# A fused decoder layer on one NeuronCore: four attention steps placed in the mixer's last part, and one causal mask made by GpSimd on the exponentials

## The chip, the core and the metric

The kernel runs on one NeuronCore of a Trainium2 chip. Five engines work side by side and meet at semaphores only: TensorE (PE, with its weight loads as PEld), VectorE (DVE), ScalarE (ACT), GpSimd (POOL) and SyncE (SP), which issues most of the DMAs. PE writes to PSUM; DVE and ACT read PSUM; POOL works on SBUF only. The metric is the device time of one execution in microseconds (us), and the number to predict is the median of the changed kernel.

## What is computed

One decoder layer for x of 8 x 256 tokens and 256 features, in float32:

```python
x = x + mixer(layernorm(x))                     # conv, gated recurrence, two gated linear maps
x = x + xattn(layernorm(x), ctx, ctx)           # 16 heads of 16
x = x + moe(layernorm(x))                       # 8 experts, top 2, capacity 641

# xattn, per batch element
scores = einsum('bhqd,bhkd->bhqk', q, k) * SCALE
scores = where(tril(ones(L, L)), scores, -inf)
probs  = softmax(scores)
out    = einsum('bhqk,bhkd->bhqd', probs, v) @ WO + bO
```

The mixer ends with `z = ssm * silu(ssm @ w2)` and `out = ssm + z @ w3`. The attention's queries come from the normalized x after the mixer, its keys and values from ctx.

## The kernel before

The program has two blocks. In each, every engine runs its own hand-written list, and a barrier of all engines stands between them.

**Block 1** (`mixer_and_projections`) takes the 2048 tokens in four blocks of 512 (`NBLK = 4`) in a loop over `i` in `range(NBLK + 2)`. Period `i` makes the recurrence, keys and values of token block `i`, the late mixer of block `i - 1` (`w2`, `gate_tanh`, `gate`, `w3`, `residual`, statistics, `normed`, `turn_q`), and the queries of block `i - 2`. The periods `i = 4` and `i = 5` have nothing new to start: they are the tail, in which only block 3's late mixer and the queries of blocks 2 and 3 are left. Matrices are split in a high and a low part, three matmuls each (`split_product`, L101). `q_high` and `biased_low` make the two parts of q, and SP stores q, k and v to DRAM (`store`, `store_v`).

**Attention** works on 16 groups g (a batch element and half its heads). `lay` loads a group's q and k from DRAM (four slots, `ITEMS`). A score unit `u = 3g + s` (48 in all) is `mask` (two matmuls, L246) and `scores` (L261) into `lead.sbanks[u % 2]`, then `maxima` on DVE (L275). After three units `turn_maxima` (L283 to L288) makes `mt`, SP stores it (`store_maxima`, L215), and `load_maxima` (L223) brings it back as two more rows of q. An attention step t then makes the scores again, turned, with the maxima taken off: `turned_mask` (L1589), `turned` (L1603) into `tbank`, `exps` on ACT (L1470) into `pr[t % 3]`, and one step later `weigh` (L1621) into `obank`. After three steps `invert` (L1839), `divide` (L1377) and `turn_back` follow, then `project` (L1641), the residual, the norm, the router and the scatter to the experts, each at a step that the tables in `attention_route_experts` name. Units run `LEAD = 6` ahead of steps: block 1's tail holds units 0 to 5, and block 2 runs `for t in range(END)` with step t and unit t + 6. Within a step the order on PE is

```python
turned_mask(t); mask(u); turned(t); scores(u); project; weigh(t - 1)
```

`turned_mask(t)` waits for `exps(t - 1)`, since there is one `tbank`. On SP, block 2 takes the groups in turn: `store_maxima(g)`, then `lay(g + 2)`, then the loads of weights and values. After the last step come the fetch of the scattered rows and the eight experts (PE nearly without a gap).

Of the kernel before, what the change touches and what calls it, by code (L numbers as in the profile page):

```python
# [14 lines left out]
P = 128  # L15
# [154 lines left out]
LEAD = 6  # L170
ITEMS = 4
# [4 lines left out]
class Lead:  # L176


    def __init__(self, nc, ctx):
# [5 lines left out]
        self.mt = [sb(f"mt{n}", [P, 32]) for n in range(2)]  # L185
        self.sbanks = [pb(f"scores{n}", [P, 8 * P]) for n in range(2)]
        piece = 4 * L
        self.q3 = [self.hi[:, n * piece:(n + 1) * piece].rearrange("p (h t) -> p h t", h=4) for n in range(ITEMS)]
        self.k3 = [self.lo[:, n * piece:(n + 1) * piece].rearrange("p (h t) -> p h t", h=4) for n in range(ITEMS)]
        self.v32 = [m[:, ITEMS * piece:(ITEMS + 1) * piece].rearrange("p (t v) -> p t v", t=2) for m in (self.hi, self.lo)]  # L190

# [46 lines left out]
def mask(pe, A, c, lead, u):  # L238

    ge(pe, A["nm"], u - 1)  # L240
    for e in range(2):
        bank = lead.sbanks[u % 2][:, e * 4 * P:(e + 1) * 4 * P]
        m = 4 if u % 3 == 0 else 2
        out = bank.rearrange("q (p k) -> q p k", p=m)
        out = out if u % 3 == 0 else out[:, :, P:2 * P]
        pe.matmul(out, c["identb"][:, :], c["mask"][:, :].unsqueeze(1).to_broadcast([P, m, P]),  # L246
                  start=True, stop=False, skip_group_check=True)


def scores(pe, A, lead, u):  # L250
# [6 lines left out]
    for p, e in todo:  # L257
# [3 lines left out]
        mm = pe.matmul(lead.sbanks[u % 2][:, at:at + keys], q[rows, p, tok], kx[rows, p, 0:keys], start=False,  # L261
# [4 lines left out]
def maxima(dve, A, lead, u):  # L266
# [3 lines left out]
    nm, sbank = lead.nm[g % 2], lead.sbanks[u % 2]  # L270
# [7 lines left out]
def turn_maxima(dve, A, own, lead, g):  # L278
# [9 lines left out]
    dve.transpose(lead.mt[g % 2][:, :], mx[:, :, :].rearrange("q n c -> q (n c)").bitcast(F32)).then_inc(A["mx"], 1)  # L288


def mixer_and_projections(nc, sems, c, lead, x_sb, bo, a, disp, qd, kd, vd, md):

    with ExitStack() as ctx:
# [16 lines left out]
        cv, th = sb("cv", [P, DC, BLK]), sb("th", [P, DC, BLK])  # L310
# [10 lines left out]
        vf = sb("vf", [P, TPB, HEADS * VP])  # L321
        banks = [m[:, n * BLK:(n + 1) * BLK] for m in lead.sbanks for n in range(2)] + [pb(f"bank{n}", [P, BLK]) for n in range(4, 8)]
# [33 lines left out]

        def pair(i, name, n):
            return banks[4 + 2 * ((len(PAIRS) * i + PAIRS.index(name)) % 2) + n]

# [9 lines left out]
        with nc.Block() as block:  # L369

            @block.sync
            def _(sp):
# [17 lines left out]
                def store(i, dst, sem, done):  # L390
                    sp.wait_ge(S[done], DC * (i + 1))
                    for e in range(2):
# [32 lines left out]
                for i in range(NBLK + 1):  # L425
# [6 lines left out]
                    if i < NBLK:  # L432
                        store(i, kd, "k_st", "kl")
                        store_v(i)
# [10 lines left out]
                lay(sp, A, S, lead, qd, kd, 1)  # L445
                load_values(sp, A, S, lead, vd, 0)
                lay(sp, A, S, lead, qd, kd, 2)
                lay(sp, A, S, lead, qd, kd, 3)
                load_values(sp, A, S, lead, vd, 1)
                store_maxima(sp, A, lead, md, 0)  # L450
                load_maxima(sp, A, lead, md, 0)
                sp.wait_ge(S["k_st"], 96 * NBLK)
# [4 lines left out]
            def _(pool):  # L457
# [37 lines left out]
                for i in range(NBLK + 2):  # L495
# [27 lines left out]
                    if i == 0:  # L523
                        other_constants(pool, S, c)

            @block.scalar
            def _(act):
# [71 lines left out]
                def ssm_high(i, m):  # L599
                    act.wait_ge(S["ssm"], DC * i + m + 1)  # L600
                    ge(act, S["q"], DC * i)
                    act.activation(xah[:, m, :], ssm[:, m, :], ACT.Copy).then_inc(S["ssmh"], 1)
# [33 lines left out]
                def q_high(i):  # L636
                    for m in range(DC):
# [22 lines left out]
                for i in range(NBLK + 2):  # L660
# [56 lines left out]
                    if last:  # L717
                        x2_high(i - 1)

            @block.tensor  # L720
            def _(pe):
# [60 lines left out]
                def w2(i):  # L782
# [5 lines left out]
                    ge(pe, S["ql"], DC * i)  # L788
                    for m in range(DC):
                        split_product(pe, pair(i + 1, "W2", m)[:, :], products("w2", m, (xah, xal))).then_inc(S["w2"], 1)  # L790

                def w3(i):
# [4 lines left out]
                    for n in range(2):  # L797
                        if i == NBLK - 1 and n == 1:
                            unit(2)
                        for j in range(2):  # L800
                            tok = slice((2 * n + j) * P, (2 * n + j + 1) * P)
                            out = pair(i + 1, "W3", n)[:, j * D:(j + 1) * D]
                            parts = []
                            for k in range(DC):
# [1292 lines left out]
```

## Time and profile before

| | us |
|---|---|
| median of 3 runs | 732.27 |
| lowest and highest | 730.75, 733.64 |
| the profiled execution | 739.06 |
| span of its instructions | 737.3 |
| PE / DVE / ACT / POOL busy | 626.5 / 501.1 / 350.2 / 333.7 |

Times in the rows below are us from the first instruction of the profiled execution, which was 6.8 us longer than the median of the runs. Block 1 without its tail ends at about 229, the tail at 269.2, the attention steps with PE's work at about 434, the last scatters at 457, and the experts fill the rest.

### The profile page before, as it was taken

How to read it: one execution, taken by the hardware profiler on the slowest of the kernel's cores; microseconds unless marked ns; L12 is line 12 of the kernel's file. 1: busy time of each engine (PE TensorE's matmuls, PEld its weight loads, DVE VectorE, ACT ScalarE, POOL GpSimd, SP SyncE). 2: the span in 40 equal slices, each digit the busy share in tenths (PEclk: the TensorE clock that was granted, in tenths of full speed). 3: DMA queues.
4: the chain of work that ended last, by engine and by line, in shares of the span. 5: the costliest groups of instructions: out<-in, count | busy, mean ns of one | idle time of the engine just before them, and what ended most of it. 6: DMA issues, size and time to landing. Idle time of an engine off the chain costs nothing.

```text
span 737.3 us, 11898 instructions
## 1 busy us (share of the span) xinstructions
PE 626.5 (85%) x4100; PEld 518.1 (70%) x4100; DVE 501.1 (68%) x1066; ACT 350.2 (48%) x683; POOL 333.7 (45%) x322
## 2 busy tenths in 40 slices
PE   3586998997987688889989851799999999999992
PEld 2465887876875554556555531799999999999992
DVE  5687688787696546666657262387888888788841
ACT  4565464662543024352343421356666666666551
POOL 1234424224240032112143367344868677686776
PEclk9798999999999669997788665699999999999997
DMA  9201403775317926556365410704263452521223
GB/s 295 83 3 43 128 29 89 274 203 139 90 44 198 211 64 164 133 141 163 83 162 142 160 38 17 254 22 152 25 170 68 127 153 43 168 31 17 28 29 44
DMA packets 63315, 81.64 MB, mean 111 GB/s; under 512 B 10295, under 2 KB 47938, under 8 KB 63256
## 3 DMA queue, kind: packets, MB, share of 16 engines
q1 hardware_dynamic: 53928, 72.85, 35.2%
q0 software_dynamic: 9216, 7.81, 7.4%
q8 instruction: 33, 0.54, 0.3%
q10 hardware_dynamic: 112, 0.23, 0.1%
q14 instruction: 26, 0.21, 0.1%
HBM read 48.27 MB, written 34.36 MB: 112 GB/s over the span
## 4 chain that ended last, share of the span: by engine, by line
PE 39%; issue 6%; DVE 5%; POOL 5%; DMA 4%; SPq 4%; ACT 1%; POOLq 0%; DVEq 0%; ACTq 0%
PE l_scores L101 13%; PE w_bank L1765 13%; DMA l_lo<-kd 3%; POOL out L1418 2%; PE a_out L1621 2%; SPq L208 2%; PE a_shared L1641 2%; POOL disp L1387 2%; PE l_scores L1699 2%; PE a_turned L1603 1%; PE l_scores L1722 1%; PE a_turned L1589 1%; PE l_scores L261 1%; DVE w_yt L1966 1%; DVE l_nm L275 1%
## 5 line engine op out<-in xcount | busy, mean ns | idle before, releaser
L1954 DVE SCALAR_TENSOR_TENSOR w_v<-w_th,l_scores 128x324 f32<-128x324 f32 x128 | 62.1, 490 | 55.1 <-ACT w_th L1509 53.8
L1509 ACT ACTIVATE w_th<-l_scores 128x324 f32<-128x324 f32 x128 | 56.4, 441 | 84.7 <-PE l_scores L101 83.8
L1405 POOL TENSOR_TENSOR l_lo<-w_v,l_hi 128x324 fp32r<-128x324 f32 x64 | 59.0, 922 | 75.0 <-ACT l_hi L1515 74.8
L1470 ACT ACTIVATE a_pr<-a_turned 128x1024 f32<-128x1024 f32 x48 | 49.1, 1023 | 89.1 <-PE a_turned L1603 87.2
L101 PE MATMUL l_scores<-l_hi,w_w1h 128*128 128x324 f32 x256 | 81.1, 317 | 2.3 <-DVE l_lo L1946 1.2
L1418 POOL DMA_INDIRECT out<-w_y,w_to x48 | 76.3, 1591 | 12.1 <-issue 9.7
L101 PE MATMUL l_scores<-l_lo,w_w1h 128*128 128x324 f32 x256 | 80.6, 315 | 0.0
L101 PE MATMUL l_scores<-l_hi,w_w1l 128*128 128x324 f32 x256 | 80.5, 314 | 0.0
L275 DVE TENSOR_REDUCE l_nm<-l_scores 128x4 f32<-128x1024 f32 (+1 forms) x48 | 58.3, 1215 | 31.7 <-PE l_scores L261 30.9
L1765 PE MATMUL w_bank<-l_hi,w_w2h 128*128 128x324 f32 x256 | 64.5, 323 | 2.2 <-DVE w_yt L1966 1.2
L1515 ACT ACTIVATE l_hi<-w_v 128x324 fp32r<-128x324 f32 x128 | 59.9, 472 | 12.4 <-DVE w_v L1954 11.7
L1928 DVE TENSOR_TENSOR w_w2l<-w_s,w_w2h 128x256 fp32r<-128x256 f32 x56 | 60.9, 1087 | 1.9
L1765 PE MATMUL w_bank<-l_hi,w_w2l 128*128 128x324 f32 x256 | 61.5, 311 | 0.0
L1765 PE MATMUL w_bank<-l_lo,w_w2h 128*128 128x324 f32 x256 | 61.5, 311 | 0.0
L1394 POOL TENSOR_TENSOR w_w1l<-w_s,w_w1h 128x256 fp32r<-128x256 f32 x64 | 55.1, 862 | 1.7 <-ACT w_w1h L1494 0.2
L1377 POOL TENSOR_TENSOR a_on<-a_po,a_rc 128x256 f32<-128x256 f32 x16 | 9.9, 620 | 98.0 <-DVE a_rc L1841 98.0
L101 PEld LDWEIGHTS l_scores<-l_hi,w_w1h 128*128 128x128 f32 x256 | 49.2, 192 | 2.9 <-ACT l_hi L1504 2.9
L101 PEld LDWEIGHTS l_scores<-l_hi,w_w1l 128*128 128x128 f32 x256 | 49.2, 192 | 0.0
L101 PEld LDWEIGHTS l_scores<-l_lo,w_w1h 128*128 128x128 f32 x256 | 49.1, 192 | 0.0
L101 PE MATMUL l_scores<-m_sh,l_hi 128*128 128x512 f32 x96 | 40.0, 416 | 10.3 <-ACT m_sh L565 6.9
L1765 PEld LDWEIGHTS w_bank<-l_hi,w_w2h 128*128 128x128 f32 x256 | 42.6, 189 | 4.1 <-issue 4.1
L1765 PEld LDWEIGHTS w_bank<-l_hi,w_w2l 128*128 128x128 f32 x256 | 43.7, 188 | 0.0
(253 smaller groups left out, 1587.0 us busy)
## 6 DMA issues: line engine op xcount, KB each, us to landing
w_s<-in_L_ffn_w SPq DMA_DIRECT2D x14, 1024.0 KB, 7.4
l_lo<-kd SPq DMA_DIRECT2D x32, 200.0 KB
l_hi<-qd SPq DMA_DIRECT2D x32, 192.0 KB
disp<-c_blank SPq DMA_DIRECT2D x8, 658.1 KB
w_rows<-disp SPq DMA_DIRECT2D x7, 658.1 KB
kd<-l_qkh SPq DMA_DIRECT2D x16, 256.0 KB, 4.7
vd<-m_vf SPq DMA_DIRECT2D x4, 1024.0 KB, 6.8
qd<-l_qkh SPq DMA_DIRECT2D x16, 256.0 KB, 3.9
```

The costliest lines, as they stand in the source:

```text
L101: mm = pe.matmul(out, a, b, start=first and n == 0, stop=last and n == 3 * len(parts) - 1)
L208: sp.dma_start(m[64 * e:64 * e + c, :, :].bitcast(F32), rows[k, e][:, :, b * L:(b + 1) * L])\
L275: dve.tensor_reduce(dst, src, AX.X, ALU.max).then_inc(A["nm"], 1)
L1394: pool.tensor_tensor(w1_piece(w1l, f), w1_piece(s1[e % 2], f), w1_piece(w1h, f).bitcast(F32), ALU.subtract)\
L1405: pool.tensor_tensor(hl[:, g % 3, half(1)], v[:, n % 4, :], hh[:, g % 3, half(1)].bitcast(F32), ALU.subtract)\
L1418: pool.indirect_dma_start(out=out, out_offset=bass.IndirectOffsetOnAxis(ap=to[:, e % 3, t:t + 1], axis=0), in_=y[e % 2][:, t, :], in_offse ...
L1470: act.activation(pr[n % 3][:, :], tbank[:, :], ACT.Exp, scale=SCALE).then_inc(A["exp"], 1)
L1509: act.activation(th[:, n % 2, :], hb[n % 2][:, 0:HALF], ACT.Tanh, scale=0.5).then_inc(F["th"], 1)
L1515: act.activation(hh[:, g % 3, half(u)], v[:, n % 4, :], ACT.Copy).then_inc(F["hh"], 1)
L1765: mm = pe.matmul(eb[2 * k + u][:, 0:HALF], w2_piece(w, f)[:, k * P:(k + 1) * P], a[:, g % 3, half(q)], start=f == 0 and n == 0, stop=f == ...
L1928: dve.tensor_tensor(w2_piece(w2l, f), w2_piece(s2[e % 2], f), w2_piece(w2h, f).bitcast(F32), ALU.subtract)\
L1954: dve.scalar_tensor_tensor(v[:, n % 4, :], th[:, n % 2, :], 1.0, hb[n % 2][:, 0:HALF], ALU.add, ALU.mult).then_inc(F["v"], 1)
```

## The change

- Four steps (`START = 4`) move into block 1's tail, and with them score units 6 to 9. Block 2 begins with step 4 and unit 10. `LEAD` stays 6.
- `turned_mask` is gone. Instead POOL zeroes what lies over the diagonal in the exponentials with an affine select (`cut`): 4 x 128 elements of each partition, and all 1024 in every third step. `weigh(n)` waits for `cut(n)` where it waited for the exponentials.
- The tail is written out by hand, in another order. Block 3's `w2` reads its input from `sh, sl`, which are free by then (before, from `xah, xal`, in which the queries of block 2 had to be done first), and the PSUM banks of the tail are dealt anew. Units 1, 3 and 5 use `tbank`, units 6 to 10 all use `sbanks[0]`.
- `pr`, `th`, `vf` and later `y` share one piece of SBUF (`area`), so that `exps(1)` waits for the store of the last values.
- SP lays groups 1 and 4 earlier, in block 1, and stores the q of block 2 in two halves around `load_maxima(0)`. The q of block 3 is stored in groups 4 and 5 of block 2, where it was the first thing of block 2.
- POOL's `with_bias` (four instructions of 128 x 1024 at the start of block 2) becomes 16 of 128 x 256, one to a step, and `base` is cut up in the same way. `cut(t)` stands first in POOL's list of step t.

```diff
+def turned(pe, A, lead, n):
+    ge(pe, A["exp"], n)
+    if n == 0:
+        pe.wait_ge(A["nm"], LEAD)
...
+def cut(pool, A, lead, n):
+    pool.wait_ge(A["exp"], n + 1)
+    own = lead.pr[n % 3][:, :].rearrange("k (m q) -> k m q", m=8 if n % 3 == 2 else 4)[:, :, 0:P]
+    pool.affine_select(out=own, in_=own, compare_op=ALU.is_ge, fill=0.0, base=0,
+                       pattern=[[0, own.shape[1]], [1, P]], channel_multiplier=-1).then_inc(A["cut"], 1)
...
 def weigh(pe, A, lead, n):
-                    pe.wait_ge(A["exp"], n + 1)
+    pe.wait_ge(A["cut"], n + 1)
...
-                for i in range(NBLK + 2):
+                for i in range(NBLK):
...
-                    if t < NS:
-                        turned_mask(t)
                     if u < NS:
                         mask(pe, A, c, lead, u)
                     if t < NS:
-                        turned(t)
+                        turned(pe, A, lead, t)
```

**PE in the tail.** In these rows `m_xah`, `m_xal` with `m_wh`, `m_wl` into two banks are a projection, L808 (L921 in the change) is `w3`, L727 (L838) is `turn_q`, and L246/L261 (L262/L277) are a score unit. Before, from the queries of block 2 to the barrier:

```order
L101 MATMUL m_bank<-m_xah,m_wh 128x512 [waits m_hs,m_xl2,m_xh2]
...
L246 MATMUL l_scores<-c_mask,c_identb 128x512 [waits m_ring]
...
L101 MATMUL m_bank<-m_xah,m_wh 128x512 [waits m_dx,m_ql,m_ssml,m_ssmh]
...
L808 MATMUL m_bank<-m_wh,m_zh 128x256 [waits m_zl,m_zh]
...
L246 MATMUL l_scores<-c_mask,c_identb 128x2x128 [waits a_nm]
...
L727 MATMUL m_bank<-c_ident,m_xn 128x128 [waits m_xn2,m_vf]
...
L101 MATMUL m_bank<-m_xah,m_wh 128x512 [waits m_hs,m_xl2,m_xh2]
...
L1577 UNCONDITIONAL_BRANCH [waits barrier_Pool_Activation_PE_DVE_SP_release]
```

The change, from `w2` of block 3 on:

```order
L101 MATMUL l_out<-m_sh,m_wh 128x512 [waits m_dx,m_vf,m_ssml,m_ssmh]
...
L921 MATMUL l_scores<-m_wh,m_zh 128x256 [waits m_ql,m_zl,m_zh]
...
L327 MATMUL l_turned<-l_hi,l_lo 128x256 [waits a_m_in0,a_nm]
L327 MATMUL l_turned<-l_hi,l_lo 128x256 x3
L838 MATMUL l_scores<-c_ident,m_xn 128x128 [waits m_xn2,m_vf]
...
L277 MATMUL l_scores<-l_lo,l_hi 128x128 [waits a_laid2]
...
L347 MATMUL l_out<-l_area,l_hi 32x256 [waits a_v_in0,a_cut]
L347 MATMUL l_out<-l_area,l_hi 32x256 x3
L101 MATMUL l_scores<-m_xah,m_wh 128x512 [waits m_xl2,m_xh2]
...
L347 MATMUL l_out<-l_area,l_hi 32x128 [waits a_cut]
```

`w2` no longer waits for the low part of block 2's queries (`m_ql`), and step 0 stands ahead of `turn_q`.

**PE in one attention step.** Before (names: `a_turned` is `tbank`, `a_out` is `obank`):

```order
L1589 MATMUL a_turned<-c_identb,c_mask 128x512 [waits a_exp]
L1589 MATMUL a_turned<-c_identb,c_mask 128x512
L246 MATMUL l_scores<-c_mask,c_identb 128x2x128 [waits a_nm]
L246 MATMUL l_scores<-c_mask,c_identb 128x2x128
L1603 MATMUL a_turned<-l_hi,l_lo 128x128 x8
L261 MATMUL l_scores<-l_lo,l_hi 128x256 x4
L1621 MATMUL a_out<-a_pr,l_hi 32x256 [waits a_exp]
```

The same step in the change:

```order
L262 MATMUL l_scores<-c_mask,c_identb 128x2x128 [waits a_nm]
L262 MATMUL l_scores<-c_mask,c_identb 128x2x128
L327 MATMUL l_turned<-l_hi,l_lo 128x128 [waits a_exp]
L327 MATMUL l_turned<-l_hi,l_lo 128x128 x7
L277 MATMUL l_scores<-l_lo,l_hi 128x256 x4
L347 MATMUL l_out<-l_area,l_hi 32x256 [waits a_cut]
```

The wait for the exponentials has moved behind `mask(u)`, and `weigh` waits for POOL.

**POOL in the steps of the change**, from the start of block 2:

```order
L1517 TENSOR_TENSOR a_on<-a_po,a_rc 128x2x8x16 [waits a_po]
L357 AFFINE_SELECT l_area<-l_area 128x4x128 [waits a_exp]
L1503 TENSOR_TENSOR g_x<-g_x,g_bo 128x256
L357 AFFINE_SELECT l_area<-l_area 128x1024 [waits a_exp]
L1503 TENSOR_TENSOR g_x<-g_x,g_bo 128x256
L357 AFFINE_SELECT l_area<-l_area 128x4x128 [waits a_exp]
L1503 TENSOR_TENSOR g_x<-g_x,g_bo 128x256
L1517 TENSOR_TENSOR a_on<-a_po,a_rc 128x2x8x16 [waits a_o,a_po]
```

Before, four additions of the bias stood here and no select.

## Rows read from the trace of the kernel before

**Rows 1.** Busy us (count) of PE, PEld, DVE, ACT, POOL by stage; clock, DMA share, GB/s.
```profile
229.10:269.20 40.10, 28.51 (x128) 21.48 (x129) 22.89 (x44) 8.70 (x13) 1.01 (x2) 0.74 0.62 154
269.20:434.50 165.30, 148.62 (x1330) 89.76 (x1330) 100.84 (x269) 64.77 (x87) 51.95 (x56) 0.82 0.53 136
434.50:463.10 28.60, 5.39 (x23) 4.17 (x23) 8.85 (x57) 2.40 (x6) 23.11 (x23) 0.53 0.15 44
```

**Rows 2.** PE in order of time: start us, us, what [idle before <-releaser].
```profile
234.91 0.47 PE L101 MATMUL m_bank<-m_xah,m_wh 128*128 128x512 f32 x1 [1.01 <-DVE m_xal L944]
...
242.15 0.55 PE L808 MATMUL m_bank<-m_wh,m_zh 128*128 128x256 f32 x1 [4.22 <-DVE m_zl L944]
...
257.09 2.21 PE L727 MATMUL m_bank<-c_ident,m_xn 128*128 128x128 f32 x8 [3.70 <-DVE m_xn L1020]
...
260.75 0.77 PE L101 MATMUL m_bank<-m_xah,m_wh 128*128 128x512 f32 x1 [0.31 <-issue]
...
269.22 0.58 PE L1589 MATMUL a_turned<-c_identb,c_mask 128*128 128x256 bf16 x2 [2.37 <-PEq L369]
...
280.67 0.39 PE L1589 MATMUL a_turned<-c_identb,c_mask 128*128 128x256 bf16 x2
```

**Rows 3.** DVE in order of time, in the tail.
```profile
228.96 0.69 DVE L914 TENSOR_TENSOR m_ssm<-m_ssm,m_dx 128x512 f32<-128x512 f32 x1
...
252.38 0.69 DVE L1013 TENSOR_TENSOR g_x<-m_bank,g_x 128x512 f32<-128x512 f32 x1 [3.18 <-PE m_bank L813]
```

**Rows 4.** Windows, columns as in group 1.
```profile
237.00:241.00 4.00, 0.93 (x5) 0.42 (x3) 2.97 (x5) 1.74 (x4) 0.00 (x0) 1.00 0.96 226
241.00:245.00 4.00, 2.85 (x13) 2.88 (x14) 2.13 (x3) 0.28 (x1) 0.00 (x0) 0.60 0.90 206
...
257.00:265.00 8.00, 7.61 (x27) 5.03 (x28) 5.14 (x8) 1.88 (x3) 0.00 (x0) 0.50 0.15 50
341.00:357.00 16.00, 16.00 (x107) 9.10 (x100) 9.28 (x32) 4.80 (x7) 1.31 (x2) 0.50 0.44 110
```

**Rows 5.** SP's queue in order of time, at the start of block 2.
```profile
283.81 3.72 SPq L1340 DMA_DIRECT2D w_wo<-in_L_xattn_WO  x8
```

**Rows 6.** The chain that ended last, in order of time, between two waits for keys.
```profile
317.31 0.73 DVE a_po L1839
...
323.69 0.56 SPq L215
...
326.47 5.15 DMA l_lo<-kd
```

**Rows 7.** PE in order of time: two waits for laid keys.
```profile
295.46 0.67 PE L261 MATMUL l_scores<-l_lo,l_hi 48*128 48x128 f32 x8 [1.00 <-DMA l_lo<-kd]
...
314.08 0.66 PE L261 MATMUL l_scores<-l_lo,l_hi 48*128 48x128 f32 x8 [0.86 <-DMA l_lo<-kd]
```

**Rows 8.** PE in order of time: one step at the full clock, one mask at half.
```profile
304.89 0.39 PE L1589 MATMUL a_turned<-c_identb,c_mask 128*128 128x256 bf16 x2 [0.26 <-ACT a_pr L1470]
305.12 0.59 PE L246 MATMUL l_scores<-c_mask,c_identb 128*128 128x512 bf16 x2
...
306.47 0.64 PE L1621 MATMUL a_out<-a_pr,l_lo 128*32 128x128 f32 x16
...
348.43 1.03 PE L1589 MATMUL a_turned<-c_identb,c_mask 128*128 128x512 bf16 x2
```

**Rows 9.** POOL's groups of lines: busy us, mean ns of one.
```profile
L1362 POOL TENSOR_TENSOR g_x<-g_x,g_bo 128x1024 f32<-128x1024 f32 x4 | 9.3, 2363 | 0.0
...
L142 POOL MEMSET c_blank<- 108x1560 f32 x1 | 1.4, 1412 | 0.0
...
L136 POOL TENSOR_SCALAR_AFFINE_SELECT c_ident<-c_ident 128x128 f32<-128x128 f32 x1 | 0.3, 288 | 0.2 <-POOL c_ident L134 0.2
```

**Rows 10.** POOL in order of time, the same subtraction twice.
```profile
208.15 1.67 POOL L476 TENSOR_TENSOR m_gl<-m_acc,m_gh 128x512 fp32r<-128x512 f32 x1
...
216.63 1.28 POOL L476 TENSOR_TENSOR m_gl<-m_acc,m_gh 128x512 fp32r<-128x512 f32 x1 [0.52 <-ACT m_gh L591]
```

More of the change, by code:

```diff
@@ L170 @@
 LEAD = 6
+START = 4
 ITEMS = 4
@@ L185, in __init__ @@
         self.mt = [sb(f"mt{n}", [P, 32]) for n in range(2)]
+        self.area = sb("area", [P, 3 * 8 * P])
+        self.pr = [self.area[:, n * 8 * P:(n + 1) * 8 * P] for n in range(3)]
         self.sbanks = [pb(f"scores{n}", [P, 8 * P]) for n in range(2)]
+        self.tbank, self.obank, self.shared = pb("turned", [P, 8 * P]), pb("out", [P, 4 * P]), pb("shared", [P, 4 * P])
         piece = 4 * L
@@ L524, in _ @@
                         other_constants(pool, S, c)
+                for t in range(START):
+                    cut(pool, A, lead, t)
             @block.scalar
@@ L891, in _ @@
                         turn_q(i - 1)
-                    if i == NBLK:
-                        unit(4)
                     if now:
                         mixed(i, 1)
+                unit(0)
+                unit(1)
+                queries(NBLK - 2, (0,))
+                w2(NBLK - 1)
+                queries(NBLK - 2, (1,))
+                unit(2)
+                unit(3)
+                w3(NBLK - 1, 0)
+                unit(4)
+                w3(NBLK - 1, 1)
+                unit(5)
+                step(0)
+                turn_q(NBLK - 1)
+                unit(6)
+                step(1)
+                weigh(pe, A, lead, 0)
+                queries(NBLK - 1)
+                step(2)
+                unit(7)
+                weigh(pe, A, lead, 1)
+                step(3)
+                unit(8)
+                weigh(pe, A, lead, 2)
+                unit(9)
             @block.vector
@@ L1091, in _ @@
                         delta(i, 2)
-                    if last and not now:
-                        for m in range(DC):
-                            last_low("ssml", xal, ssm, xah, "ssmh", i - 1, m)
-                    if i == NBLK:
-                        maxima(dve, A, lead, 0)
                     if i + 1 < NBLK:
@@ L1109, in _ @@
                         dmin(i, 3)
-                    if last and not now:
-                        for m in range(DC):
-                            last_low("zl", zl, z, zh, "zh", i - 1, m)
-                    if i == NBLK:
-                        maxima(dve, A, lead, 1)
                     if now:
@@ L1443, in _ @@
                 low_w1(0, FC - 1)
-                base(NBLK - 2)
-                base(NBLK - 1)
+                for t in range(TPB * (NBLK - 2), NT):
+                    base(t)
                 low(0)
@@ L1973, in result @@
                         .then_inc(F["y_dve"], 1)
-                for t in range(END):
+                invert(0)
+                for t in range(START, END):
                     u = t + LEAD
```

333 lines of the change are left out of this document (189 added, 144 removed).

## The prediction

> **What bounds the kernel now.** I read the windows by stage first, then PE in order of time through the tail, then the chain that ended last through the attention steps, then POOL's groups. The windows [rows 1] show three stages that the change can touch. In the tail PE is busy 28.5 of 40.1 us at a mean clock of 0.74. In the attention steps it is busy 148.6 of 165.3 us at 0.82. In the routing's end, 28.6 us, POOL is busy 23.1 and PE 5.4. The experts behind that get the same work in the same order; I leave them as they are.
>
> PE in the tail [rows 2] is bound by a chain through all engines: `w2` waits for the low part of ssm (starts at 234.91), `w3` for the low part of z (242.15, after 4.22 us idle), `turn_q` for the normalized x (257.09, after 3.70), the last queries start at 260.75, and block 2 starts at 269.22. Step 4 starts at 280.67. So the first four steps stand on this path with 280.67 - 269.22 = 11.45 us, while the tail has holes of about that size.
>
> The clock matters there. PE was nearly idle from 237 to 241, the clock went from 1.00 to a mean of 0.60 in the next four us, and at 0.50, which is 1.2 GHz, eight us of nearly full PE work still ran from 257 to 265 [rows 4]. `w3` and its residual took 242.15 to 253.07, or 10.9 us [rows 2, 3].
>
> In the attention steps the chain that ended last does not run through PE alone. It passes DVE (the turn of `obank`, x, statistics, two maxima) from 317.31, SP's store of the maxima at 323.69 and then four lay DMAs whose last takes 5.15 us, to 331.6 [rows 6]. PE waits for such keys until 295.46 and until 314.08, 1.00 and 0.86 us [rows 7]. Other cycles are bound by PE itself: from 341 to 357 it is busy 16.00 of 16.00 us at half clock [rows 4].
>
> **The change, part by part.**
>
> *The tail's front.* The last sum of ssm ends at 228.96 + 0.69 = 229.65 [rows 3]. Its high part on ACT and its low part on DVE are instructions of about 0.65 us each (128 x 512, as the 0.69 of that row), so both are there at about 231.1. `w2` in the change waits for these and no longer for block 2's queries, of which half (six matmuls) stand ahead of it on PE; I start it at 231.3, which is 234.91 - 231.3 = 3.6 us earlier. From `w2` to `w3` it took 242.15 - 234.91 = 7.2 us; the same steps follow each other, so `w3` starts at 238.6.
>
> *`w3` at the full clock.* PE's hole before `w3` is now filled by half the queries and units 2 and 3, with 1 to 1.5 us idle left. The clock had held through 241 with four us of near-idleness, so I take `w3` and units 4 and 5 at 2.4 GHz. The 10.9 us go to about 6.4 (40 matmuls and a unit at half their time, and 0.69 of residual): x is done at 245.0, 8.1 us earlier.
>
> *Norm and turn.* From x to `turn_q` it took 257.09 - 253.07 = 4.0 us. In the change one `maxima` and `turn_maxima` stand on DVE ahead of the normalization, of which some 0.6 us is not covered by POOL's power: 249.7. Step 0 needs the same maxima and fits in this hole.
>
> *The work put in.* `turn_q` and half a us of copies take 2.2 at half clock (PE has been idle from 244.8 to 248.5). Then unit 6, step 1 and `weigh(0)` stand ahead of the last queries: about 1.8 + 0.8 + 1.1. They start at 255.5 where they started at 260.75: 5.2 of the 8.1 us are left. The queries are 12 matmuls, 2.8 us at 2.4 GHz and 5.1 at 1.2. Behind them q's two parts (0.7 each), and a strict alternation of PE and DVE, because units 7, 8 and 9 share one bank: `maxima(7)`, unit 8, `maxima(8)`, unit 9, `maxima(9)`, which is 3 x 1.2 + 2 x 1.1 with the gaps. The sum is 255.5 + 4.0 + 1.4 + 5.8 = 266.7. All at the full clock it would be 265.7, all at half 270.3. Step 4 starts at 266.8 where it started at 280.67: **13.9 us**, with ends at 10.4 and 15.
>
> SP must follow. In block 2 it issues the first weights, the maxima of group 2, the 3.72 us of WO [rows 5], and only then lays group 5: 266.7 + 1.1 + 0.6 + 4.2 + 0.6 + 2.9 + 5.1 = 281.2 for the scores of unit 15. (1.1 and 0.6, 0.5 and 0.6 are its short issues, 2.9 and 5.1 the lay.) In the trace this was at 295.46, after 1.00 us of waiting [rows 7], so the 14 us stand. PE waits here some 3 us now.
>
> *The masks of turned scores.* At the full clock the next instruction starts 305.12 - 304.89 = 0.23 us after one of 2 x 256 columns [rows 8], twice that for 2 x 512; at half clock twice as much again (the 1.03 us row). All 44 left in block 2 give 44 / 3 x 0.9 = 13 us at the full clock. But only cycles bound by PE can pay. Between two waits for keys of odd groups the path goes DVE, SP, DMA [rows 6], in which no mask stands: zero. I count the masks of twelve steps at half clock in two PE-bound cycles, 2 x 2.5, and 3 for the nine last steps, most of them held by other engines; less 2 us because the wait before unit 15 leaves the clock low. **6 us**, ends 0 and 10.
>
> *The select on POOL.* The trace has a select of 128 elements only: 0.288 us. A memset runs at 1.412 / 1560 = 0.9 ns an element, an addition of two inputs at 2.363 / 1024 = 2.3 [rows 9]. That puts 512 elements at 0.63 to 1.2 us, and 1024 at 1.1 to 2.4. I take 0.8 and 1.5, near the select's own row. The exponential's end to `weigh` on PE is 306.47 - 304.89 + 0.26 = 1.8 us before, of which the two masks leave (about 0.75): 1.1 in the change. The short select is done in time, the long one costs 0.5 us of PE's wait in every third step. It is partly covered, since `turned(t + 1)` waits for the exponential of step t anyway. I take zero beyond what the range holds. The Trainium skill, "GPSIMD Engine Reference", section "Performance versus the Vector engine", gives about 1.8 cycles an element as the best case of a loop with one input, 0.77 us for 512; as an estimate that would be 1.5 us for 1024, and the sum by it is the same. No row here has that size.
>
> *`with_bias` and `base` in pieces, q stored later, keys 1 and 4 earlier.* POOL is busy 52 of 165 us in the steps [rows 1]; 44 selects add about 45, with room. The additions of bias go from 9.3 us in one piece to 16 pieces, of which one stands between two selects. SP's stores of q moved behind two lays: nobody waits until group 12. Zero each; uncovered, a late select would cost PE its length.
>
> *Sum.* 739.06 - 13.9 - 6 = 719.2 for a profiled execution. This one was 6.8 us over the median, and rows do not tell where. If the median run has no half clock in `w3`, 4.5 us of my gain are not there; I take half of that back: 732.27 - 19.9 + 2.2 = **714.5 us**.
>
> **Rivals.** *The lay chain takes the masks' gain.* PE gets faster and waits as much longer for keys. For it: the waits [rows 7], and the 8 us from `turn_maxima` to the scores hold no PE work [rows 6]. Against: the sixteen us of saturated PE [rows 4]. 714.5 + 5 = 719.5.
>
> *The tail is longer.* The clock falls in the hole before step 0 and stays at half through units 6 to 9: block 2 starts at 270.3, 3.5 us later, and step 0 waits for the round trip of the maxima, about 2 more: 720.
>
> *The port.* The same subtraction on POOL took 1.67 us beside a DVE scan and 1.28 without [rows 10]. A select that is stretched by 0.4 us in each group's long step costs 16 x 0.3 = 5 us: 719. The Trainium skill, "SBUF — State Buffer", section "Who interferes with whom", says that a DVE instruction with two SBUF inputs and a GpSimd one shut each other out for their whole length. The trace agrees in size, but in the steps DVE reads mostly PSUM.
>
> *Slower: the select holds PE and takes its clock.* If 1024 elements cost 2.4 us, `weigh` waits 1.4 us in every third step, PE loses the density that keeps 2.4 GHz, and the groups that now run at full clock (about eight, 7.1 us each) run like those at half (11 less the masks' 1.7, so 9.4): +18 us; projections and the rest of these steps +5. Less the 14 us of the tail and without the masks' 6: 732.3 - 13.9 + 23 = 741. It decides from about 2 us for the long select. Against it: the 0.288 us row.
>
> *The change does not do it* (steps 0 to 3 wait in the tail for their maxima and push it back by as much): 11.45 us return, only some masks stay: 728.
>
> **How the numbers follow.** Forecast 0.55, lay chain 0.14, long tail 0.13, port 0.06, no effect of the tail 0.06, slower 0.06. The forecast's own ends: 732.27 - 15 - 10 = 707 and 732.27 - 10.4 - 2 + 4.5 = 724. The rivals to 720 lie inside; I go to 705 and 727. Half a per cent, 3.7 us, is about what a measurement can tell from no change: 728.6 is the bound. Faster 0.91, same 0.03, slower 0.06.
>
> **What would show it.** Right: `w2` at 231 to 232; `w3` at 238 to 240 at a clock of 1.00 with x done by 246; block 2's first PE work at 266 to 270 with step 4; long selects of 1.2 to 1.8 us; PE's waits for `kd` longer than before; the experts' length unchanged. Wrong: a PE wait on POOL as a leading row of the waits; block 2 starting after 272; a granted clock in the steps well below 0.82.

## The result, and the profile after

The changed kernel takes **747.4 us** (median of 4 runs, 744.0 to 749.6) where the kernel before takes 732.5 in the runs beside it: the ratio is 1.020, with a 95% interval of 1.016 to 1.025. I had forecast 714.5, between 705 and 727. It is slower, and lies outside the range. The profiled execution took 749.57 us, its span is 747.8. Runs that were clearly longer than the others of their kernel, at a lower granted clock, are left out of the ratios; the profiled run of the kernel before (739.1) is one of them, so its rows are set below beside those of k7, the same kernel with one store moved, profiled at 730.1.

The windows by stage, columns as in [rows 1]:

```profile
229.10:268.30 39.20, 31.07 (x209) 21.62 (x206) 28.71 (x53) 13.48 (x17) 4.15 (x6) 0.87 0.65 163
268.30:443.50 175.20, 142.54 (x1142) 86.08 (x1142) 103.68 (x254) 60.72 (x83) 89.28 (x117) 0.66 0.47 124
443.50:472.00 28.50, 6.81 (x34) 5.41 (x30) 10.40 (x65) 2.40 (x6) 21.32 (x24) 0.56 0.09 24
```

The tail holds four steps more in 39.2 us, at a clock of 0.87 where it was 0.74. The attention steps, four fewer of them, take 175.2 us instead of 165.3, and the clock in them is 0.66 instead of 0.82. (From 268 to 343 and from 343 to 408 us it is 0.67 and 0.66; k7 has 0.89 and 0.87 there.) The routing's end is as long as before, and the experts behind it take 275.8 us instead of 274.2. Nearly the whole loss is in the steps.

PE through the tail, in order of time, as [rows 2]:

```profile
231.93 0.39 PE L101 MATMUL l_out<-m_sh,m_wh 128*128 128x512 f32 x1
...
239.07 0.36 PE L921 MATMUL l_scores<-m_wh,m_zh 128*128 128x256 f32 x1 [0.98 <-ACT m_zh L708]
...
249.07 0.50 PE L327 MATMUL l_turned<-l_hi,l_lo 50*128 50x256 f32 x4 [3.59 <-DVE l_nm L291]
250.12 2.21 PE L838 MATMUL l_scores<-c_ident,m_xn 128*128 128x128 f32 x8 [0.55 <-DVE m_xn L1155]
```

`w2`, `w3` and `turn_q` start within 0.7 us of the forecast (231.3, 238.6, 249.7), and in the windows from 237 to 249 the clock is 1.00. Block 2's first PE work, the mask of unit 10, stands at 268.27. The tail did what it was meant to.

The exponential of one step is a milestone that both kernels have. Steps 4, 24, 26, 37, 40 and 47, first in the kernel before, then in the changed one (ACT in order of time):

```profile
281.76 1.02 ACT L1470 ACTIVATE a_pr<-a_turned 128x1024 f32<-128x1024 f32 x1 [1.14 <-PE a_turned L1603]
343.66 1.02 ACT L1470 ACTIVATE a_pr<-a_turned 128x1024 f32<-128x1024 f32 x1 [4.12 <-PE a_turned L1603]
350.98 1.02 ACT L1470 ACTIVATE a_pr<-a_turned 128x1024 f32<-128x1024 f32 x1 [2.76 <-PE a_turned L1603]
392.56 1.02 ACT L1470 ACTIVATE a_pr<-a_turned 128x1024 f32<-128x1024 f32 x1 [2.13 <-PE a_turned L1603]
402.31 1.02 ACT L1470 ACTIVATE a_pr<-a_turned 128x1024 f32<-128x1024 f32 x1 [2.55 <-PE a_turned L1603]
429.07 1.00 ACT L1470 ACTIVATE a_pr<-a_turned 128x1024 f32<-128x1024 f32 x1
```

```profile
269.12 1.02 ACT L365 ACTIVATE l_area<-l_turned 128x1024 f32<-128x1024 f32 x1 [5.06 <-PE l_turned L327]
339.09 1.02 ACT L365 ACTIVATE l_area<-l_turned 128x1024 f32<-128x1024 f32 x1 [2.94 <-PE l_turned L327]
349.61 1.01 ACT L365 ACTIVATE l_area<-l_turned 128x1024 f32<-128x1024 f32 x1
390.06 1.03 ACT L365 ACTIVATE l_area<-l_turned 128x1024 f32<-128x1024 f32 x1 [1.69 <-PE l_turned L327]
410.81 1.02 ACT L365 ACTIVATE l_area<-l_turned 128x1024 f32<-128x1024 f32 x1 [6.07 <-PE l_turned L327]
437.77 1.00 ACT L365 ACTIVATE l_area<-l_turned 128x1024 f32<-128x1024 f32 x1
```

The lead is 12.6 us at step 4, 4.6 at step 24, 1.4 at step 26, 2.5 at step 37, and a lag of 8.5 at step 40 and 8.7 at step 47. Against k7, whose profiled run is at its median, the leads are 15.2 and 3.1 at steps 4 and 24, and the lags 2.7, 5.8, 16.7 and 16.9 at the other four: 32 us lost between step 4 and step 47, of which 12 by step 24. So there are two losses of different kinds: a slow one over the first twenty steps, and sharp ones near steps 26 and 39.

The sharp ones are read from PE's waits and from SP's queue. PE first, from 268 to 443 us (what waited <- what it waited for: us in total, times, longest):

```profile
PE l_turned L327 <- DMA l_hi<-md: 14.7, 5, 6.6
```

```profile
353.04 0.80 PE L327 MATMUL l_turned<-l_hi,l_lo 50*128 50x256 f32 x4 [5.03 <-DMA l_hi<-md]
...
402.58 0.80 PE L327 MATMUL l_turned<-l_hi,l_lo 50*128 50x256 f32 x4 [6.60 <-DMA l_hi<-md]
```

Step 27 waits 5.03 us for the maxima of group 9, step 39 later 6.6 for those of group 13. Now DVE (where those maxima are made), SP and POOL around it, in order of time:

```profile
338.08 0.21 DVE L304 STREAM_TRANSPOSE l_mt<-l_mx 128x32 f32<-128x32 f32 x1
```

```profile
345.38 0.39 SPq L1465 DMA_DIRECT2D out<-g_x  x1
345.81 0.57 SPq L231 DMA_DIRECT2D md<-l_mt  x1
```

```profile
334.91 0.73 POOL L1512 TENSOR_TENSOR g_x<-g_x,w_x 128x256 f32<-128x256 f32 x1
...
344.62 0.74 POOL L1512 TENSOR_TENSOR g_x<-g_x,w_x 128x256 f32<-128x256 f32 x1
```

The maxima are ready at 338.3 (338.08 and 0.21). SP stores them at 345.81, since `store_base(0)` stands ahead in its queue and waits for four pieces of `base`. The change dealt these pieces out to steps 22 to 25, one each (the first and the last stand above), and the last ends at 345.36. SP's wait for POOL there lasts 16.3 us, and the next such store is late too, at 394.53: the maxima of group 13, ready at 385.4, follow it at 394.97. In the kernel before, with `base` in one piece, SP issued that store at 339.64 and the maxima at 340.71.

The slow loss goes with the clock. Windows right behind the start of block 2, columns as in [rows 1]:

```profile
265.00:269.00 4.00, 1.93 (x18) 1.18 (x20) 2.93 (x6) 0.00 (x0) 0.19 (x1) 1.00 0.34 84
269.00:273.00 4.00, 4.00 (x37) 2.07 (x34) 2.94 (x4) 1.02 (x1) 1.95 (x3) 0.64 0.40 100
...
277.00:281.00 4.00, 4.00 (x32) 2.14 (x28) 2.74 (x5) 1.02 (x1) 2.69 (x5) 0.50 0.86 188
281.00:285.00 4.00, 4.00 (x30) 2.13 (x28) 2.52 (x4) 1.73 (x3) 2.46 (x3) 0.50 0.17 45
285.00:289.00 4.00, 4.00 (x16) 2.69 (x18) 1.23 (x1) 0.93 (x2) 1.32 (x2) 0.50 0.52 124
```

PE idled half of the four us up to 269; its clock fell to 1.2 GHz and stayed there from 273 to 289, although PE is busy nearly all of that time. A stretch like this is no proof by itself: k7, with its masks on PE, was granted 0.50 from 273 to 281 and 0.51 from 281 to 285 with PE busy 4.00 us in each window of four. The difference is in how often it happens, which the means over the steps show. The select itself is cheap (POOL's groups, busy us and mean ns):

```profile
L357 POOL TENSOR_SCALAR_AFFINE_SELECT l_area<-l_area 128x512 f32<-128x512 f32 x32 | 20.5, 642 | 28.0 <-ACT l_area L365 27.8
L357 POOL TENSOR_SCALAR_AFFINE_SELECT l_area<-l_area 128x1024 f32<-128x1024 f32 x16 | 17.5, 1093 | 25.4 <-ACT l_area L365 25.3
```

So two theories stood: **A**, SP's queue (the sharp losses), and **B**, the clock without the masks on PE (the slow loss). Within B it was open whether the added PE work counts or the new wait of `weigh` for POOL.

### The profile page after: what moved, and what is told of

Same layout as the page of the kernel before. It is cut to its first block, busy times and chain, and to the rows that moved or that the text cites. A ratio compares the mean times of both kernels' runs of the same rounds, so it can differ in the third digit from the quotient of the medians.

```text
span 747.8 us, 11802 instructions
## 1 busy us (share of the span) xinstructions
PE 626.7 (84%) x4004; PEld 517.2 (69%) x4004; DVE 511.0 (68%) x1066; ACT 353.1 (47%) x685; POOL 375.0 (50%) x394
## 4 chain that ended last, share of the span: by engine, by line
PE 39%; POOL 7%; DVE 6%; issue 6%; DMA 3%; ACT 1%; SPq 1%; POOLq 0%; ACTq 0%; DVEq 0%
PE l_scores L101 13%; PE l_turned L1857 6%; PE l_out L1857 3%; PE l_shared L1857 3%; PE l_shared L1733 2%; PE l_out L347 2%; POOL disp L1527 2%; POOL out L1558 2%; PE l_scores L1791 2%; DMA l_lo<-kd 2%; PE l_turned L327 2%; PE l_scores L277 1%; PE l_scores L1814 1%; POOL l_area L357 1%; PE l_scores L262 1%
## 5 line engine op out<-in xcount | busy, mean ns | idle before, releaser
L365 ACT ACTIVATE l_area<-l_turned 128x1024 f32<-128x1024 f32 x48 | 49.1, 1023 | 98.9 <-PE l_turned L327 95.8
L1558 POOL DMA_INDIRECT out<-l_area,w_to x48 | 76.2, 1588 | 12.1 <-issue 9.7
L291 DVE TENSOR_REDUCE l_nm<-l_scores 128x4 f32<-128x1024 f32 (+1 forms) x45 | 54.8, 1217 | 37.1 <-PE l_scores L277 37.0
L1654 ACT ACTIVATE l_hi<-w_v 128x324 fp32r<-128x324 f32 x128 | 59.9, 472 | 12.4 <-DVE w_v L2044 11.8
L357 POOL TENSOR_SCALAR_AFFINE_SELECT l_area<-l_area 128x512 f32<-128x512 f32 (+1 forms) x48 | 38.0, 792 | 53.4 <-ACT l_area L365 53.2
L327 PEld LDWEIGHTS l_turned<-l_hi,l_lo 50*128 50x128 f32 x256 | 24.5, 250 | 38.0 <-issue 29.1
L327 PE MATMUL l_turned<-l_hi,l_lo 50*128 50x256 f32 (+1 forms) x256 | 34.8, 382 | 18.3 <-DMA l_hi<-md 14.7
L101 PE MATMUL l_scores<-m_sh,l_hi 128*128 128x512 f32 x96 | 40.0, 417 | 10.3 <-ACT m_sh L657 6.9
L566 POOL TENSOR_TENSOR m_gl<-m_acc,m_gh 128x512 fp32r<-128x512 f32 x16 | 24.5, 1533 | 37.4 <-ACT m_gh L683 37.4
L557 POOL TENSOR_TENSOR m_rstd<-m_ve,c_mhalf 128x4 f32<-128x4 f32 (+1 forms) x7 | 8.3, 1189 | 62.7 <-DVE m_ve L118 62.7
L101 PE MATMUL l_scores<-m_sl,l_hi 128*128 128x512 f32 x96 | 39.2, 408 | 0.0
```

What stands on the lines that cost most here:

```text
L101: mm = pe.matmul(out, a, b, start=first and n == 0, stop=last and n == 3 * len(parts) - 1)
L291: dve.tensor_reduce(dst, src, AX.X, ALU.max).then_inc(A["nm"], 1)
L327: mm = pe.matmul(lead.tbank[:, at:at + w], kx[rows, p, key], q[rows, p, tok], start=True, stop=True, skip_group_check=True)
L365: act.activation(lead.pr[n % 3][:, :], lead.tbank[:, :], ACT.Exp, scale=SCALE).then_inc(A["exp"], 1)
L1558: pool.indirect_dma_start(out=out, out_offset=bass.IndirectOffsetOnAxis(ap=to[:, e % 3, t:t + 1], axis=0), in_=y[e % 2][:, t, :], in_offse ...
L1654: act.activation(hh[:, g % 3, half(u)], v[:, n % 4, :], ACT.Copy).then_inc(F["hh"], 1)
```

## The experiments

### First four: each suspect alone, and both

**k1_store_later**: the changed kernel, with the store one group later.

```
-                    if g % 4 == 0 and g >= 8:
+                    if g % 4 == 1 and g >= 9:
                         store_base(g // 4 - 2)
```

> The changed kernel with one thing moved: SP issues the two stores of the first 1024 output rows (store_base(0), store_base(1)) one group later (groups 9 and 13, behind that group's store of the maxima). Theory A, SP's queue: in the changed kernel store_base(0) waits until 345.38 for the fourth piece of base on POOL (16.3 us at the longest), and the store of the maxima of group 9, ready since 338.3, is issued at 345.81; the same at 394.97. Then the waits of PE for md of 5.03 and 6.60 us go, and the time falls from 747.4 by 10 to 13 us to 734-737. Theory B, the clock: PE at a mean clock of 0.66 is the bound through the steps and the waits for md only take the place of slower PE work; then 743-747.

Measured: **731.5** (10 runs, 726.4 to 736.1), ratio to before 1.000 (0.997 to 1.004). 15.8 us less than the changed kernel. SP, in order of time:

```profile
336.50 0.57 SPq L231 DMA_DIRECT2D md<-l_mt  x1
...
343.44 0.38 SPq L1465 DMA_DIRECT2D out<-g_x  x1
```

The maxima leave first, and PE's waits for `md` shrink (again from 268 to 443 us):

```profile
PE l_turned L327 <- DMA l_hi<-md: 3.5, 5, 1.2
```

Theory A holds, and is worth more than I expected (734 to 737). The waits for `md` are 11.2 us shorter; where the rest of the 15.8 comes from is not shown.

**k2_pe_masks**: the changed kernel, its masks of turned scores again on PE, no select.

```
-    pe.wait_ge(A["cut"], n + 1)
+    pe.wait_ge(A["exp"], n + 1)
...
-                    if t < NS:
-                        cut(pool, A, lead, t)
...
+                    if t < NS:
+                        turned_mask(pe, A, c, lead, t)
```

The same is done in the tail's four steps.

> The changed kernel with the causal mask of the turned scores back on PE (two bf16 matmuls a step, the turned scores accumulate onto them) and no select on POOL; weigh waits for the exponential. The tail with four steps stays, SP's order stays. Theory B, the clock: the dense bf16 columns give back the granted clock, the mean in the steps rises from 0.66 to 0.8 and the 8 us lost between step 4 and step 24 come back: about 739. Theory A, SP's queue: base is still in pieces that end at step 25, so the two long waits for md stay; PE has 48 x 0.3 to 0.8 us more work: 745-752.

Measured: **737.8** (8 runs, 734.4 to 739.2), 9.6 us less than the changed kernel, and the clock in the two windows is 0.89 and 0.72 where that kernel has 0.67 and 0.66. Theory B holds beside A, with its two halves (the work on PE, the wait for the select) still together.

**k3_both**: both edits.

> Both edits: SP's store of the base one group later, and the masks of the turned scores back on PE. If A and B both hold, the 12.4 us that the tail gained are all kept: 732.5 - 12 = 720 (718-724). If only A holds: 736-740, no better than the store alone. If only B holds: 739 as with the masks alone.

Measured: **719.8** (4 runs, 718.3 to 725.3), ratio 0.986 (0.981 to 0.992). Step 4's exponential is at 266.70 and the last at 408.63. It beats both kernels, and the two causes about add up: 15.8 and 9.6 one by one, 27.6 together.

**k4_cut_alone**: the kernel before with the select (and pieces, and the later store), its tail as it was.

```
+                    if t < NS:
+                        cut(t)
...
-                    if t < NS:
-                        turned_mask(t)
```

> The kernel before, its tail untouched, with the select on POOL instead of the masks on PE, with_bias and base in pieces as in the changed kernel, and SP's store of the base one group later. It shows the select's half of the change without the tail and without SP's wait. Theory B (without the masks the clock falls): 738-742, clock in the steps about 0.7. Theory A alone (the select is free or a gain, the loss was SP's queue): 727-733.

Measured: **742.8** (4 runs, 736.6 to 744.3), ratio 1.013 (1.007 to 1.019): 11.8 us slower than before, just above what theory B expected. The select's half of the change is a loss by itself, whatever the tail does.

### Which half of the masks' removal costs

**k5_masks_and_cut**: k1 with the two mask matmuls issued for nothing; the turned scores overwrite them. The same line stands ahead of the tail's four steps.

```
+                    if t < NS:
+                        turned_mask(pe, A, c, lead, t)
                     if u < NS:
                         mask(pe, A, c, lead, u)
                     if t < NS:
                         turned(pe, A, lead, t)
```

> The changed kernel with SP's store of the base one group later, and the two bf16 mask matmuls of every step issued again on PE where they stood before, without use: the turned scores overwrite them, and POOL's select stays. Beside the store alone (731.5) it adds only PE work; beside masks on PE with no select (719.8) it adds only the select and weigh's wait for it. Theory B1, the clock: the loss without the masks comes from PE's lower granted clock; then the added work makes it faster, 720-724, clock in the steps 0.85 to 0.9. Theory B2, the select's wait: the loss comes from weigh waiting for POOL behind the exponential; then 731-737, no faster for more PE work.

**k6_no_mask_no_cut**: k1 with neither the mask matmuls nor the select. It leaves out the causal mask of the weights altogether, and serves as a measure of time only.

> The changed kernel with SP's store of the base one group later and the causal mask of the turned scores left out altogether: neither the matmuls on PE nor the select on POOL, weigh waits for the exponential (keys after the query get their weight too). Theory B1, the clock: the select costs nothing and its absence gives nothing, 728-732, clock in the steps about 0.7. Theory B2, the select's wait: with the wait gone and less PE work it is the fastest of all, 710-717.

Measured: k5 **724.7** (4 runs, 722.5 to 726.7), k6 **727.5** (5 runs, 725.1 to 728.5). With k1 and k3 this is a square:

| | no select | select on POOL |
|---|---|---|
| masks on PE | 719.8 (k3) | 724.7 (k5) |
| no masks on PE | 727.5 (k6) | 731.5 (k1) |

Down a column, less work on PE costs 7.7 and 6.8 us. Along a row, the select costs 5.0 and 4.0. k1 and k3 ran beside one set of runs of the kernel before, k5 and k6 beside another; the ratios to it are 0.986 (0.981 to 0.992), 0.989 (0.985 to 0.993), 0.993 (0.989 to 0.997) and 1.000 (0.997 to 1.004) for k3, k5, k6 and k1. By these the masks are worth about 5 and 8 us, the select 2 and 5. Only the 8, k5 against k1, is clear of the noise by itself; the direction of the select's cost is supported by PE's waits below and by k11. k5 lies just above what the clock theory expected (720 to 724), k6 just below (728 to 732), and both far from the other theory, which had 731 to 737 and 710 to 717. So less work on PE costs time, and it is the larger part of B; the clock theory's claim that the select costs nothing is not borne out. The same two windows of each kernel (268 to 343 and 343 to 408 us, columns as in [rows 1]), k1, k6, k5, k3:

```profile
268.00:343.00 75.00, 64.82 (x562) 38.33 (x558) 50.65 (x99) 28.02 (x36) 41.08 (x58) 0.73 0.57 140
343.00:408.00 65.00, 56.54 (x457) 34.47 (x455) 46.84 (x119) 24.99 (x34) 36.25 (x46) 0.68 0.50 128
```

```profile
268.00:343.00 75.00, 68.69 (x580) 40.44 (x574) 49.37 (x107) 28.36 (x37) 24.09 (x36) 0.70 0.59 148
343.00:408.00 65.00, 57.72 (x455) 35.95 (x457) 39.69 (x111) 26.04 (x36) 24.93 (x30) 0.69 0.54 147
```

```profile
268.00:343.00 75.00, 65.99 (x681) 40.31 (x684) 57.02 (x113) 30.51 (x40) 43.24 (x61) 0.96 0.60 150
343.00:408.00 65.00, 57.25 (x493) 34.53 (x489) 42.43 (x107) 26.26 (x37) 38.78 (x48) 0.81 0.54 154
```

```profile
268.00:343.00 75.00, 67.70 (x675) 41.02 (x672) 52.91 (x113) 30.12 (x39) 24.21 (x36) 0.92 0.61 153
343.00:408.00 65.00, 58.40 (x508) 35.03 (x510) 39.73 (x123) 26.88 (x38) 25.95 (x32) 0.80 0.51 148
```

Without the masks the clock is 0.68 to 0.73 with or without the select; with them it is 0.80 to 0.96. This doesn't hang on one profile each: over whole executions the clock is 0.892 or more in every run of the five kernels with both masks on PE once a step (before, k2, k3, k5, k7), and 0.889 or less in every run of the five without (the changed kernel, k1, k4, k6, k8). PE's busy time hardly differs. What differs is how fast the same instruction runs. The larger group of the projection's matmuls on PE, in the changed kernel and in k3 (behind the bar: busy us in total, mean ns of one); a second group of eight does not differ, 638 and 654 ns:

```profile
L1733 PE MATMUL l_shared<-w_wo,a_ot 128*128 128x256 f32 x48 | 20.1, 591 | 0.0
```

```profile
L1735 PE MATMUL l_shared<-w_wo,a_ot 128*128 128x256 f32 x48 | 14.0, 442 | 0.0
```

All selects together take 38 us. What of them reaches PE in k1 is this wait:

```profile
PE l_out L347 <- POOL l_area L357: 4.8, 6, 3.0
```

It comes partly from what POOL has queued ahead of the select. The longest of the six is near the end; POOL and PE in order of time:

```profile
421.20 0.73 POOL L1508 TENSOR_TENSOR w_rstd<-w_ve,c_mhalf 128x2 f32<-128x2 f32 x1 [0.85 <-DVE w_ve L118]
421.91 0.71 POOL L1534 TENSOR_TENSOR w_w1l<-w_s,w_w1h 128x256 fp32r<-128x256 f32 x1
422.80 1.05 POOL L1527 DMA_INDIRECT disp<-w_x,w_si  x1 [0.18 <-issue]
423.87 0.65 POOL L357 TENSOR_SCALAR_AFFINE_SELECT l_area<-l_area 128x512 f32<-128x512 f32 x1
```

```profile
424.58 1.08 PE L347 MATMUL l_out<-l_area,l_lo 128*32 128x256 f32 x8 [3.01 <-POOL l_area L357]
```

The exponential of that step had ended at 420.3; the select took its turn behind a power, a low part and a scatter.

### The store and the pieces

**k7_before_store_later**: the kernel before, with k1's edit alone.

> The kernel before with SP's store of the base one group later and nothing else. In its trace the maxima of groups 9 and 13 wait at most 1 us behind that store (out<-g_x issued at 339.64 and 386.98, the maxima at 340.71 and 387.48), so it should be within 2 us of before: 729-732. Then the 11.3 us of the tail and masks-on-PE kernel are the tail's alone. If it gains 5 us or more, part of them is SP's order.

Measured: **730.1** (10 runs, 725.6 to 736.2), ratio 0.998 (0.994 to 1.001): no difference. SP's order is worth nothing that can be measured where `base` is one piece, so the difference of k3 to k7, 10.3 us (about 9 by their ratios to the kernel before), is that of the tail together with the rest of the change: k3 also has the additions in pieces, the earlier keys and the later store of q, which no run takes apart.

**k8_base_whole**: the changed kernel with `base` in one piece, SP's order untouched.

```
-                    for i, first in enumerate(BASE):
-                        if first <= t < first + TPB:
-                            base(TPB * i + t - first)
+                    if t in BASE:
+                        base_whole(BASE.index(t))
```

> The changed kernel with base again as one addition of 128x1024 at steps 22 and 34, as before, and SP's order as in the changed kernel. Theory A (SP's store waits for the fourth piece, which POOL does only in step 25): the wait of SP shrinks from 16 us to about 9 and the long waits of PE for md go, as with the store moved: 731-736. Against it: a whole base of 2.4 us stands between two selects and holds weigh in two steps, +1 to 2 us. If the pieces are not what makes the store late: 745-748.

Measured: **733.4** (10 runs, 728.0 to 738.8), 14.0 us less than the changed kernel. SP's two longest waits for `base`, in the changed kernel and in k8:

```profile
SPq L1465 <- POOL g_x L1512: 30.2, 2, 16.3
```

```profile
SPq L1465 <- POOL g_x L1517: 17.0, 2, 8.7
```

Taking away either the pieces or the place of the store in SP's queue removes the loss. That settles theory A.

### More, less, twice

**k9_half_fill**: k5 with one useless mask matmul a step instead of two (`for e in range(1)`).

> As the kernel with useless masks on PE and the select on POOL (724.7), but with one of the two useless mask matmuls a step instead of two. Beside 0 (731.5) and 2 (724.7). Theory B1, the clock: PE's added work buys granted clock, and half of it buys part: 726-730, clock in the steps between 0.69 and 0.85. If the gain comes from something else that the two matmuls do (the wait for the exponential standing ahead of the next mask and scores, that is another order), one matmul does it as well as two: 723-725.

Measured: **730.8** (10 runs, 723.8 to 734.4). The median says that one matmul does nothing beside none (731.5), the windows of its profiled run, which is the fastest of the ten, show a clock between:

```profile
268.00:343.00 75.00, 67.84 (x608) 40.72 (x608) 53.44 (x106) 29.31 (x38) 42.31 (x59) 0.81 0.59 146
343.00:408.00 65.00, 56.89 (x507) 34.77 (x505) 43.21 (x113) 26.49 (x37) 39.04 (x48) 0.79 0.55 155
```

Its other nine runs have a clock between as well: 0.886 to 0.902 over the whole execution, with medians of 0.880 for k1 (none), 0.895 for k9 (one) and 0.916 for k5 (two). Counted by the span of the instructions alone, the medians are 729.8, 727.8 and 723.0 us. The other reading, that the gain comes from the order, expected 723 to 725: k9's waits and order are those of k5, and its median doesn't reach that. The clock theory had 726 to 730. But the ten runs spread over 10.6 us, so how the gain grows with the work stays open.

**k10_double_fill**: k3 with each mask matmul issued twice (`for e in (0, 1, 0, 1)`).

> As the kernel with both edits (719.8: masks on PE, store later, no select), with each mask matmul issued twice, the second time overwriting the first with the same values: 4 mask matmuls a step instead of 2. Its clock in the steps is at 0.83 to 0.98 already, so there is little left to buy, and the added work (48 x 0.5 us at full clock = 24 us) lies on PE: theory B1 expects 724-735, slower. If more PE work still gains, the clock was not near its top: below 719.

Measured: **719.6** (4 runs, 717.5 to 722.5), the same as k3. My expectation of 724 to 735 fell. The clock of the second window rose from 0.80 to 0.91, and the added work costs nothing that can be measured (the ratios to the kernel before are 0.979, 0.972 to 0.987, and 0.986 for k3):

```profile
268.00:343.00 75.00, 70.47 (x688) 43.18 (x688) 50.69 (x109) 29.32 (x38) 24.29 (x36) 0.92 0.59 149
343.00:408.00 65.00, 60.50 (x565) 37.73 (x564) 40.19 (x111) 27.26 (x39) 24.99 (x30) 0.91 0.56 155
```

**k11_cut_twice**: k1 with every select done twice.

```
+    for _ in range(2):
+        ge(pool, A["half_cut"], 2 * n + _)
...
-    pe.wait_ge(A["cut"], n + 1)
+    pe.wait_ge(A["half_cut"], 2 * n + 2)
```

> As the changed kernel with the store one group later (731.5), with every select on POOL done twice, the second on the result of the first: 1.3 us for 128x512 and 2.2 us for 128x1024, the length that the slower rival of the prediction asked for. Without any select this kernel takes 727.5, so the first one costs 4 us of the 38 us that all take. If a select is mostly covered, the second costs about as much again or somewhat more: 736-742. If the rival's threshold is real (from 2 us on PE waits in every third step and loses its clock further): 748 or more, clock in the steps below 0.65.

Measured: **741.9** over all five runs (732.4 to 743.9), 740.0 without the two that its ratio leaves out, 1.011 (1.004 to 1.018). That is 8 to 10 us over k1, where the first select costs about 4: the cover runs out, within what the covered select expected (736 to 742). PE's waits for the select:

```profile
PE l_out L347 <- POOL l_area L359: 14.4, 14, 3.7
```

They are 9.6 us longer than in k1. The profiled run was the fastest of the five; its clock, 0.76 and 0.65 in the two windows, isn't clearly below k1's. The other four have 0.858 to 0.868 over the whole execution, though, below every run of k1 (0.874 to 0.889), so part of the loss may be clock, and the two are not taken apart. The rival's threshold (748 or more from about 2 us) was not seen.

## Why the prediction was wrong

The four terms, as the runs have them, from 730.1 (k7) up to the changed kernel: the tail -10.3 (k3), the masks off PE +7.7 (k6), the select +4.0 (k1), SP's queue +15.8. They are differences along one chain of kernels, so that they add up to 747.4 is arithmetic and confirms nothing. What does: k4, which makes the middle two steps on the old tail (with the additions in pieces), loses 11.8 us by them, where they are 11.7 here. The first term holds the rest of the change as well, and the third is about as small as the noise.

*What bounds the kernel.* Right that three stages matter and that the loss or gain had to show in the first two. I noted that from 341 to 357 PE was busy 16.00 of 16.00 us at half clock [rows 4] and took from it only that these cycles were bound by PE. The same row says that busy time there is not work at full speed, and that in this stage the clock is something to win or to lose.

*The tail's front, `w3` at the full clock, norm and turn, the work put in.* Right, place by place: 231.93, 239.07, 250.12, and block 2 at 268.27 where I had 266.8. The size was a little off: 12.4 us earlier than [rows 2] instead of 13.9. Measured in whole runs it is 10.3, just under my lower end of 10.4. I had written that these us stand. Against k7, k3 is 17.6 us ahead at the exponential of step 4 and 12.3 at the last (408.63 and 420.88): some 5 us of the lead go on the way, and where is not shown.

*The masks of turned scores.* This is the first step that failed, and in its sign: -6 us forecast, with ends at 0 and 10, +7.7 measured. I took the price of the masks from their durations [rows 8] and asked how many of them lie on PE's path. I didn't ask what the clock does when they are gone. I had the mechanism in hand: I subtracted 2 us for a clock left low by one wait, and in the slower rival PE "loses the density that keeps 2.4 GHz". But I made that depend on the select's length. Here the clock went down with the masks and came back with them, useful or not. Ends at "0 and 10" for an edit that takes work from a clocked engine were too narrow below.

*The select on POOL.* The price was right or better: 0.64 us for 512 elements against 0.8, 1.09 for 1024 against 1.5. Both lie on the lower ends that I had worked out, 0.63 and 1.1. That it costs nothing was wrong by some 4 to 5 us, as near as the runs can tell. "POOL with room" is a mean; the select stands in a queue behind other work, and the room is not where the exponential ends.

The Trainium skill, "GPSIMD Engine Reference", section "Performance versus the Vector engine", gives 0.77 us for 512 elements at 1.8 cycles an element; as an estimate by the same figure, 1024 would take 1.5. The measured ones are shorter, and they decide.

*`with_bias` and `base` in pieces, q stored later.* The second step that failed, and the most expensive: zero forecast, +15.8 measured. I asked only who waits on POOL for the pieces' time (PE, through a late select). I didn't ask who waits for the last piece. That is SP, in order, with the maxima of the next group queued behind. [rows 6] shows the path DVE, SP, DMA as the one that ended last, so a wait put ahead of SP's store of maxima had to reach the path: 7.5 us of lateness at SP became 5.03 us of PE's waiting at step 27. I asked what is queued behind a waiting POOL and a waiting PE, and not what is queued behind a waiting SP.

*The 2.2 us taken back* for the difference of the profiled run to the median: of no weight, and not tested.

*The rivals.* The slower one had 741 and a chance of 0.06; the time came out 6 us above even that, so the direction was in my list and the reason was not. Its effect came (a clock of 0.66 in the steps, one of my signs of being wrong), its cause did not: the long select took 1.09 us, not 2.4. k11, with the length it asked for, takes 8 to 10 us more than k1, and not the 23 that the rival reckoned. The lay chain, the long tail and the port didn't show as terms. I had given longer waits of PE for `kd` as a sign of a right forecast; in the steps they are 1.2 us in all, less than the 5.6 before. In k3 and k5, where PE's clock is higher, they are 4.0 and 5.2: a slower PE leaves the lays time.

*The chances.* 0.91 for faster rested on two zeros that I hadn't bounded. A rival in which a wait moves to SP had no place in the list.

## What to carry to other kernels

Before work is taken off TensorE, read its granted clock in that stage: where it hovers between its levels, as here, fewer matmuls can make the others slower, and useless ones may be free or better; try it, since one useless matmul a step gained nothing clear here and two gained 7 us. When an instruction is split into pieces spread over later steps, its consumers wait for the last piece; follow that wait into an in-order DMA queue and see what stands behind it. Mean idle time of an engine is no cover for an instruction on a short loop between two others.

## What the runs showed of the hardware

- Useless work made the kernel faster: k5 issues 96 matmuls more than k1, whose results are overwritten, and takes 6.8 us less. k10 issues twice k3's masks and takes the same time.
- A PE that is busy 4.00 of 4.00 us was granted 0.50 for three windows in a row (277 to 289 in the changed kernel; k7, with the masks on PE, has the like from 273 to 285). The Trainium skill, "TensorE: Matmul & The Clock Gate", section "What's actually happening", says that the clock follows how busy the PE has been of late. The traces agree that it falls behind an idle stretch (265 to 269). That busy time as the profile counts it does not bring it back at once is seen in both kernels; in the changed one it came back to a mean of 0.80 from 289 to 293.
- Over whole executions the clock goes with the mask matmuls in each step: 0.880 with none (k1), 0.895 with one (k9), 0.916 with two (k5), and in the kernels without a select 0.880 with none (k6), 0.915 with two (k3), 0.933 with four (k10).
- The select on GpSimd ran at 0.64 us for 128x512 and 1.09 for 128x1024 in f32: (1093 - 642) / 512 is 0.88 ns an element, with 0.19 us fixed. From 128 elements, 0.288 us [rows 9], the same line gives 0.30.
